# Storing pairs of accumulator sets while the graph matrices are built

## What is computed

```
C[source, target] = number of edges from source to target      (layers 1 and 3)
W[source, target] = sum of edge_weight over those edges        (layer 4)
```

## Time and profile before

| | us |
|---|---|
| median of 3 runs | 2702.98 |
| lowest and highest of them | 2699.75, 2709.37 |
| the profiled execution | 2699.71 |
| its span in the trace | 2697.9 |
| build stage, first one-hots to the next stage's first work | 54 to 549 of the span |

### The profile page before, as it was taken

The page is one execution under the profiler, slowest core; times in us unless marked ns, Lnnn a source line. Parts: engine busy times, 40 slices in busy tenths (PEclk is TensorE's granted clock), DMA queues, the critical chain, the costliest instruction groups (busy, mean ns, idle before and its releaser), DMA issues. The chain is left out here.

```text
span 2697.9 us, 55857 instructions
## 1 busy us (share of the span) xinstructions
PE 2221.2 (82%) x18268; PEld 2088.8 (77%) x18269; DVE 1638.3 (61%) x3181; ACT 1356.5 (50%) x2800; POOL 1111.1 (41%) x1225
## 2 busy tenths in 40 slices
PE   2878788869999999687778877788788748779998
PEld 1877777869999999487677777777777648779998
DVE  7888778855433334566565666666666664465465
ACT  1666556643333332165555555555555523257686
POOL 2655556500000000277777777777777702200000
PEclk6999999989999999765555555555555569979999
DMA  1444444410000000444444444444444452096281
GB/s 58 143 131 128 133 128 141 135 45 2 2 2 1 2 2 16 118 118 116 108 113 113 109 117 108 111 115 109 117 109 110 109 213 104 2 385 226 79 292 39
DMA packets 184980, 283.92 MB, mean 105 GB/s; under 512 B 76675, under 2 KB 152678, under 8 KB 179270
## 3 DMA queue, kind: packets, MB, share of 16 engines
q1 hardware_dynamic: 145958, 200.50, 23.4%
q0 software_dynamic: 38688, 79.28, 11.5%
HBM read 210.52 MB, written 69.15 MB: 104 GB/s over the span
## 5 line engine op out<-in xcount | busy, mean ns | idle before, releaser
L1238 POOL DMA_INDIRECT layer_R<-source_terms,layer_srcs x800 | 781.7, 977 | 243.7 <-issue 243.7
L1470 PE MATMUL layer_zp<-layer_right,layer_left 96*128 96x192 f32 x1342 | 471.3, 536 | 178.9 <-DVE layer_left L1257 174.8
L1470 PEld LDWEIGHTS layer_zp<-layer_right,layer_left 96*128 96x128 f32 x1342 | 404.1, 327 | 195.7 <-DVE layer_left L1257 186.7
L1004 PEld LDWEIGHTS layer_acc<-layer_U,graph_CT 128*128 128x128 f16 x6250 | 524.7, 97 | 30.6 <-ACT layer_U L933 21.1
L1004 PE MATMUL layer_acc<-layer_U,graph_CT 128*128 128x192 f16 (+1 forms) x6250 | 529.8, 246 | 22.0 <-ACT layer_U L933 20.0
L573 PE MATMUL build_win<-build_M,build_S 128*128 128x200 f16 x3948 | 382.6, 253 | 127.3 <-DVE build_S L504 77.0
L573 PEld LDWEIGHTS build_win<-build_M,build_S 128*128 128x128 f16 x3948 | 335.3, 99 | 156.9 <-issue 45.6
L1491 PEld LDWEIGHTS layer_acc<-layer_hot,layer_G 128*98 128x98 f32 x1648 | 252.3, 256 | 114.9 <-DVE layer_aggT L1311 114.8
L1491 PE MATMUL layer_acc<-layer_hot,layer_G 128*98 128x32 f32 x1648 | 268.3, 329 | 54.0 <-DVE layer_aggT L1311 53.8
L2209 PE MATMUL layer_acc<-layer_V,layer_turn 128*128 128x96 f32 x2500 | 287.9, 278 | 0.6 <-issue 0.6
L2209 PEld LDWEIGHTS layer_acc<-layer_V,layer_turn 128*128 128x128 f32 x2500 | 286.0, 195 | 0.9 <-issue 0.9
(11 more groups left out here) (312 smaller groups left out, 2890.4 us busy)
## 6 DMA issues: line engine op xcount, KB each, us to landing
layer_ring<-W_blocks SPq DMA_DIRECT2D x41, 1600.0 KB, 8.3
W_blocks<-nodes_x SPq DMA_DIRECT2D x400, 100.0 KB, 2.3
layer_left<-in_attr SPq DMA_DIRECT2D x68, 384.0 KB
layer_C<-C_blocks SPq DMA_DIRECT2D x25, 800.0 KB, 19.8
layer_R<-source_terms,layer_srcs POOLq DMA_INDIRECT x800
C_blocks<-nodes_x SPq DMA_DIRECT2D x13, 800.0 KB, 4.9
C_blocks<-build_Cblk SPq DMA_DIRECT2D x12, 800.0 KB, 4.8
layer_rows<-target_rows SPq DMA_DIRECT2D x68, 96.0 KB
```

The source lines that it names most:

```text
L1004: return pe.matmul(acc[:, k % RING, 0:columns], CT[:, t, k * P:(k + 1) * P], pairs[:, cur, t, 0:columns], start=(t == 0), stop=(t == NT - 1))
L1238: nc.gpsimd.indirect_dma_start(R[:, i, u, :], None, P_d, bass.IndirectOffsetOnAxis(ap=at_u, axis=0)).then_inc(s_R[i], 16)
L1470: pe.matmul(out[u], left[:, i, u * P:(u + 1) * P], right[:, i, :], start=(u % 2 == 0), stop=False, skip_group_check=True)
```

## The change

ScalarE now copies two accumulator sets in one operation: 400 columns of C, then 400 columns of W. The W buffers become three of two windows each (`Wtwo`). They are used in the fixed order `WSLOT` = 0, 1, 2, 0, 1, 2, 0, 1 within each node tile. SyncE stores a pair of windows with one transfer of 200 KB. The count `s_evac` rises by 2 for each of these copies, TensorE's wait for a free set is made only before even windows and asks for the pair that ended two windows earlier, and the wait before the transposes follows. To make room, `tab` moves into an unused row of `CT` and `sw` into the tensor `ident`, which is written again by the next stage. GpSimd's extra call of `columns` after the loop goes.

```diff
+WSLOT = (0, 1, 2, 0, 1, 2, 0, 1)
-        tab = m.sb("tab", [1, NG + 1, GW + 2], I16)
+        tab = CT[0:1, NT - 1, 3 * ETK:3 * ETK + TAB].bitcast(I16).rearrange("p (q b) -> p q b", b=GW + 2)
-        sw = m.sb("sw", [P, SWB, PARTS, GT, 2], F16)
+        sw = later[:, 0:SWB * PARTS * GT].bitcast(F16).rearrange("p (r a t z) -> p r a t z", r=SWB, a=PARTS, z=2)
-        Wwin = words[:, CW:CW + 4 * WC].rearrange("p (r c) -> p r c", r=4)
+        Wtwo = [words[:, CW + 2 * WC * r:CW + 2 * WC * (r + 1)] for r in range(2)] + [m.sb("Wtwo", [P, 2 * WC], F32)[:, :]]
...
-            columns(0, NG)
...
-                    sp.wait_ge(s_evac, j * (2 * WPT) + 2 * u + 2 + EVAC0)
-                    sp.dma_start(W_d[bass.ds(j, 1), :, u * WC:(u + 1) * WC].rearrange("o p c -> p (o c)"),
-                                 Wwin[:, u % 4, :]).then_inc(s_wst[u % 4], 16)
+                    if u % 2 == 1:
+                        sp.wait_ge(s_evac, j * (2 * WPT) + 2 * u + 2 + EVAC0)
+                        sp.dma_start(W_d[bass.ds(j, 1), :, (u - 1) * WC:(u + 1) * WC].rearrange("o p c -> p (o c)"),
+                                     Wtwo[WSLOT[u // 2]]).then_inc(s_wst[WSLOT[u // 2]], 16)
...
-                    pe.wait_ge(s_evac, j * (2 * WPT) + 2 * WPT + EVAC0 - 1)
+                    pe.wait_ge(s_evac, j * (2 * WPT) + 2 * WPT + EVAC0 - 2)
...
-                        pe.wait_ge(s_evac, 2 * w + 1)
+                        if i % 2 == 0:
+                            pe.wait_ge(s_evac, 2 * w + 3)
...
-                for u in range(WPT):
-                    act.wait_ge(s_built, j * WPT + u + 1 + 2 * GW)
-                    nc.scalar.activation(Cblk[b][:, :, u * WIN:(u + 1) * WIN],
-                                         win[:, u % 4, 0:WC].rearrange("p (d k) -> p k d", d=WIN),
-                                         ACT.Copy, scale=0.5).then_inc(s_evac, 1)
-                    act.wait_ge(s_wst[u % 4], j * 64 + u // 4 * 16 + 1)
-                    nc.scalar.activation(Wwin[:, u % 4, :], win[:, u % 4, WC:2 * WC], ACT.Copy).then_inc(s_evac, 1)
+                for u in range(0, WPT, 2):
+                    act.wait_ge(s_built, j * WPT + u + 2 + 2 * GW)
+                    both = slice(u % 4, u % 4 + 2)
+                    nc.scalar.activation(Cblk[b][:, :, u * WIN:(u + 2) * WIN].rearrange("p k (w d) -> p w k d", w=2),
+                                         win[:, both, 0:WC].rearrange("p w (d k) -> p w k d", d=WIN),
+                                         ACT.Copy, scale=0.5).then_inc(s_evac, 2)
+                    r, done = WSLOT[u // 2], WSLOT[:u // 2].count(WSLOT[u // 2])
+                    act.wait_ge(s_wst[r], j * (16 * WSLOT.count(r)) + 16 * done + 1)
+                    nc.scalar.activation(Wtwo[r].rearrange("p (w c) -> p w c", w=2), win[:, both, WC:2 * WC],
+                                         ACT.Copy).then_inc(s_evac, 2)
                     if before and u % GW == 2:
                         turned(j - 1, u // GW)
```

More of the change, by code:

```diff
@@ L322, in _, with build_matrices @@
                                         add, None, ALU.add).then_inc(s_tables, 1)
-def build_matrices(nc, tab_d, pair_d, key, smod, weight, CT, indeg, spare, C_d, W_d):
+def build_matrices(nc, tab_d, pair_d, key, smod, weight, CT, indeg, spare, later, C_d, W_d):
     NCOL = 3
@@ L333, in build_matrices @@
         m = Scope(nc, ctx, "build")
-        tab = m.sb("tab", [1, NG + 1, GW + 2], I16)
+        TAB = (NG + 1) * (GW + 2)
+        tab = CT[0:1, NT - 1, 3 * ETK:3 * ETK + TAB].bitcast(I16).rearrange("p (q b) -> p q b", b=GW + 2)
         colsM = m.sb("colsM", [P, HALF, 2], F16)
@@ L373, in build_matrices @@
         s_cst = [m.sem(f"C_stored{b}") for b in range(2)]
-        s_wst = [m.sem(f"W_stored{r}") for r in range(4)]
+        s_wst = [m.sem(f"W_stored{r}") for r in range(3)]
         block = ctx.enter_context(nc.Block())
@@ L472, in _ @@
                 sp.wait_ge(s_cst[b], 16 * (NT // 2 + 1 - b) + 1)
-            for r in range(4):
-                sp.wait_ge(s_wst[r], 16 * (NW // 4) + 1)
+            for r in range(3):
+                sp.wait_ge(s_wst[r], 16 * NT * WSLOT.count(r) + 1)
         @block.vector
@@ L2249, in gnn @@
                 edge_ranges(nc, src_cols, dst_cols, dst_rows, w_cols, tab_d, tabs_d, base_d, row_d, pair_d, key, smod, weight, unscale, CT)
-                build_matrices(nc, tab_d, pair_d, key, smod, weight, CT, indeg, xs, C_d, W_d)
+                build_matrices(nc, tab_d, pair_d, key, smod, weight, CT, indeg, xs, ident, C_d, W_d)
             propagate(nc, x, xs, CT, indeg, src_cols, We, be, Wn, bn, ident, first, P_d, Q_d)
```

## The result

The changed kernel is slower: 2717.41 us median of 7 runs (2714.55 to 2721.2) against 2702.98 for the kernel before in the same comparison, a ratio of 1.0048 [1.0034, 1.0063]; in a second comparison (e9 below) the ratio is 1.0027 [1.0014, 1.0041]. Its profiled execution took 2714.55 us, with a span of 2712.8. The forecast of 2699.5 and its range of 2688 to 2711 missed it on the slow side.

What follows compares the result with a forecast made beforehand. The prediction took VectorE's cycle to set the build stage's pace. A 3.3 us gain, all other parts zero, took the median from 2703.0 to 2699.7, rounded to 2699.5; the 8-in-10 range was 2688 to 2711.

Steps and rivals of the forecast that it cites:

- ScalarE's waits for W stores: Build stage: most of the 82.0 us in 101 waits should vanish, with far less reaching the path.
- The copies: ScalarE's two-set copies: 512 ns each (bounds 343 and 822), its busy time falling by 68 us, hidden.
- The release of the sets: Accumulator pairs come free about 1.2 us after their last matmul; TensorE needs 2.04 us per pair, so cost zero.
- the event at 298: ScalarE's copy at 297.57 waited 3.56 us for a W store behind the C store; its removal gives back 2.5 us.
- Rival C: 200 KB stores land too late at a tile's end, ScalarE then TensorE and VectorE wait: 2712 us; chance 0.10.
- Rival A: The 1.2 us at each VectorE loop turn is really TensorE held up by ScalarE: 29 us more go, 2671; chance 0.08.
- D: Rival: ScalarE's wait for stores is on the path in full, so 82 us go: 2621 us; chance 0.02.
- the three signs of being wrong: Waits at each fourth group shrink; five TensorE stops fall below 5.5 us; ScalarE waits for stores at each tile's start.
- The rest: Remaining parts, such as GpSimd's call and moved buffers: 0; TensorE's five stops vary by themselves, some 3 us either way.
- Rival B: TensorE's stops at its loop's turn shorten because SyncE issues half the requests: 11 us in all, 2692; chance 0.10.
- the cost of the loop's turn: VectorE's first group of each four begins about 1.2 us late, 24 times, 29 us; expected to stay.
- The forecast gain: Fewer store waits reaching the path: 2.5 us from one large event plus 0.8 from four small ones, bounds 0 and 5.3.

Runs made afterwards that it cites:

- e9: The changed kernel measured once more, nothing altered: 2717.14 us, 1.0027 of the kernel before.
- e1: Changed kernel, but SyncE issues the C store only once TensorE has built the next node tile's first window: 2699.31 us, 0.9982 of the kernel before.
- e10: Changed kernel with the C store held and ScalarE copying one accumulator set at a time, stores still in pairs: 2705.56 us, 0.9985 of the kernel before.
- e12: Changed kernel with the C store held and VectorE's loop body made of 20 groups instead of 4: 2686.37 us, 0.9912 of the kernel before.
- e3: Changed kernel, but ScalarE copies one accumulator set at a time, stores still in pairs: 2708.71 us, 1.0007 of the kernel before.
- e4: Changed kernel plus eight unused transposes at the head of each node tile: 2704.59 us, 0.9998 of the kernel before.
- e6: Kernel before with only the moved buffers and without GpSimd's extra call: 2709.75 us, 1.001 of the kernel before.
- e11: Changed kernel with the C store held and eight unused transposes at the three of four tile heads not behind a stop: 2700.74 us, 0.9969 of the kernel before.
- e8: Changed kernel without W stores inside the build stage (W filled afterwards with other data): one run, sequence 484.0 us, no total time given.
- e5: Changed kernel with the C store held and eight unused transposes at every node tile's head: 2700.38 us, 0.999 of the kernel before.

## Why the prediction was wrong

**What held.** ScalarE's waits for W stores were off the path: 82 us of them went, and the time rose. The copies take 0.50 us (512 ns forecast). The release of the sets stayed hidden: e1 and e10 agree, and apart from the five stops and the group behind each no first matmul of the changed kernel starts more than 0.25 us after its operands; at 300.35, near the place of the event at 298, it is 0.14 (operands ready at 300.21). Rival C did not happen: ScalarE waited 0.3 us for stores, which land in 2.4 us (forecast 2.7):

```profile
DMA to landing us min/median/max: 1.9/2.4/4.7
```

Rival A is refuted by e12. The 1.2 us belong to VectorE's loop, as the prediction said, and go with its turns. D was 82 us away. None of the three signs of being wrong appeared: the prediction had named no way for these waits to grow. One size was off without an effect on the time: ScalarE's busy time fell by 37 us instead of 68, because copies that follow each other directly overlap (in the kernel before three of them start at 187.59, 187.81 and 188.02, each 0.34 to 0.36 long).

The Trainium skill (Perfetto Trace Analysis, Optimizing Scalar/DVE Operations) holds out that, where ScalarE isn't saturated but causes bubbles on other engines, breaking up its instructions may let work finish sooner. No run here shows it: in e10 the copies were split and nothing came of it, and e3's small gain is unexplained.

**The step that failed** is "The rest". It let TensorE's stops vary by 1.2 us "by themselves" and booked five of them at 3 us either way. Some of that is free (5.32 to 6.33 in e1), but each stop ends with a code packet, and an early C store delays it. They grew by 6.1 us, and VectorE's waits behind them by 7.2. Rival B looked at the right place with the wrong sign. It counted the requests that SyncE no longer issues, and did not ask when the C store behind them would go out: freed of its backlog, SyncE sends 800 KB 2 to 4 us earlier, into the stop. The prediction named the backlog, and that is the question that it should have led to: what comes earlier now, and what does it collide with?

**The turn of VectorE's loop** was taken as fixed at about 1.2 us, "the cost of the loop's turn". It ends with two 8 KB packets, a fetch too, and a 200 KB store issued some 3.0 to 3.25 us ahead of the turn lengthens it by 0.4 against a turn of the same kernel without one. That is 3.4 us (4.8 without the event at 298, which the kernel before has in this row).

**The clock** has no step in the prediction. TensorE's idle time of up to 1.9 us at the heads of tiles stood in the timeline of the kernel before; that a little more of it would cost the clock was not considered. The row "others" grew by 6.7 us (by 4.9 in e9), and e4 gives it back.

**The forecast gain** of 3.3 us is lost in these losses. Its 2.5 us came from one event in one execution, and e6 shows that such events come and go: there VectorE's three waits behind them are 11 us, where the execution that the prediction read has one of 2.60. Both bounds of that term, 0 and 5.3, were drawn from one trace. In the two profiles of the changed kernel no such event stands, which may be why the medians differ by less than the two sequences; no run isolates it.

The Trainium skill (Runtime: NRT & Kernel Launch, Instruction fetch mechanics) says that a taken branch to code outside the pages held forces a DMA fetch before execution goes on. The trace agrees in kind, with 1.2 to 1.5 us from the landing to TensorE's first matmul and 1.9 to VectorE's first operation. The page speaks of blocks of 16 KiB; here q8 moves 16 KB and q14 8 KB.

**What stays open.** The clock did not fall behind each long idle time: in e10 18 matmuls behind 2.22 us run at 111 ns, while behind 2.00 us in the changed kernel they take 161; and in the changed kernel itself they take 98 behind 2.01 us (at 445.68). What else decides was not tried. Nor was a version that has e11's transposes and e12's loop body together. The sizes of the three losses rest on one or two recorded executions each.

## What to carry to other kernels

When a change empties a queue, list what then goes out earlier and what will be under way at that moment: here the relief of SyncE moved a large store into a code fetch. A wait at the turn of a long loop body that names no releaser, or has one length whatever releaser it names, may be a fetch; look for packets of the instruction queues beside it, keep large stores away from it, and try a longer body with fewer turns. A wait that vanishes off the path may have been the spacing that kept transfers apart.

## What the runs showed of the hardware

- A turn of TensorE's loop body of four node tiles costs 5.1 to 8.0 us, and ends 1.2 to 1.6 us after a 16 KB instruction packet lands. That packet begins 2.7 to 4.3 us into the stop in the kernel before, e1 and e6, and 4.4 to 5.7 us in 19 of 20 stops into which an 800 KB store was sent after 1.2 to 2.1 us (after, e3, e8, e9).
- A turn of VectorE's body of four groups costs 1.1 to 1.9 us where it waits for nothing else. A body five times as long needs 80 packets instead of 125 for the same groups, and 4 turns instead of 24.
- TensorE's clock fell to its 1.2 GHz level behind idle times of about 2 us between bursts of matmuls, 0.1 to 0.4 us longer than those at the same heads in the kernel before, behind which it had stayed at 2.4 GHz. It didn't fall behind each such time (2.22 us in e10). Eight small transposes in the idle time kept it up at every such head in e4, and at all but one in e5 and in e11.
